# A fused attention and feed-forward kernel: the third query head's matmuls and rotation stand behind the first score tiles

## The reference

```
q = (layernorm(x) @ wq)      # 32 query heads of 128
k, v = ctx @ wk, ctx @ wv    # 8 key/value heads, each shared by 4 query heads
q, k = rope(q), rope(k)      # x * cos + rotate_half(x) * sin
attn = softmax(q @ k.T / sqrt(128) + mask)
x = x + (attn @ v) @ wo
```

## Time and profile before

| | |
|---|---|
| median of 3 runs | 760.55 us (760.4 to 761.59) |
| profiled execution, own time | 761.71 us |
| its span, first to last instruction | 759.7 us |
| mean granted TensorE clock | 0.966 of full speed |
| TensorE matmul busy | 686.3 us, 90% of the span |
| VectorE busy | 546.6 us, 72% |
| ScalarE busy | 365.8 us, 48% |
| GpSimd busy | 434.2 us, 57% |
| span covered by the attention | about 233 to 650 us |

### The profile page before, as it was taken

The page is one execution under the profiler, slowest core; times in us unless marked ns, Lnnn a source line. Parts: engine busy times, 40 slices in busy tenths (PEclk is TensorE's granted clock), DMA queues, the critical chain, the costliest instruction groups (busy, mean ns, idle before and its releaser), DMA issues.

```text
span 759.7 us, 10849 instructions
## 1 busy us (share of the span) xinstructions
PE 686.3 (90%) x3104; PEld 500.8 (66%) x3104; DVE 546.6 (72%) x1057; ACT 365.8 (48%) x685; POOL 434.2 (57%) x387
## 2 busy tenths in 40 slices
PE   4699679797766899999999999999999999599998
PEld 1244234344335678888888888888888888478886
DVE  6877629978785788888888888787888887631112
ACT  1277404246332675656666666566666564031111
POOL 1655505383243786667666766667676544536672
PEclk9899879899998999999999999999999999899999
DMA  8744504321400122121211212212112002203221
GB/s 335 258 146 130 186 1 138 104 78 56 152 28 28 57 98 69 57 70 41 82 42 57 81 39 86 68 42 59 66 41 83 28 15 98 83 2 121 86 83 55
DMA packets 37162, 63.58 MB, mean 84 GB/s; under 512 B 3216, under 2 KB 11536, under 8 KB 36112
## 3 DMA queue, kind: packets, MB, share of 16 engines
q1 hardware_dynamic: 37136, 63.26, 25.8%
HBM read 53.81 MB, written 9.44 MB: 83 GB/s over the span
## 4 chain that ended last, share of the span: by engine, by line
PE 73%; DVE 17%; issue 5%; ACT 3%; POOL 1%; DMA 1%; POOLq 0%; ACTq 0%; DVEq 0%
PE ps L502 15%; PE ps L504 15%; PE ps L503 15%; PE ps L564 10%; PE ps L531 7%; PE ps L409 5%; DVE mx_amax L1041 2%; DVE mx_raw L1054 2%; PE ps L459 1%; DVE f L1083 1%; DVE f_amax L1078 1%; DVE stats L962 1%; PE ps L385 1%; DVE k_cos L1073 1%; PE ps L418 1%
## 5 line engine op out<-in xcount | busy, mean ns | idle before, releaser
L888 POOL TENSOR_SCALAR prob<-prob,rinv 128x512 f32<-128x512 f32 x128 | 89.0, 696 | 122.3 <-DVE rinv L1198 122.2
L754 ACT ACTIVATE prob<-ps,nmax 128x512 f32<-128x512 f32 x128 | 88.3, 690 | 62.8 <-DVE nmax L1191 60.5
L765 ACT CAST pT<-ps 128x512 fp32r<-128x512 f32 x128 | 75.1, 587 | 81.5 <-PE ps L531 80.7
L564 PE MATMUL ps<-xt,wq_sb 128*128 128x512 f32 x384 | 106.0, 402 | 6.1 <-DVE q_cos L1206 3.0
L1191 DVE CUSTOM_DVE_ANT_0 ps<-ps,mask_sb 128x512 f32<-128x512 f32 x128 | 88.3, 690 | 17.7 <-PE ps L504 16.7
L409 PE MATMUL ps<-ctxT,wk_sb 128*128 128x512 f32 x128 | 66.6, 679 | 28.1 <-DVE k_cos L1073 14.1
L1212 DVE TENSOR_TENSOR pT<-ps,pT 128x512 fp32r<-128x512 f32 x128 | 86.9, 679 | 4.7 <-ACT pT L765 1.7
L564 PEld LDWEIGHTS ps<-xt,wq_sb 128*128 128x128 f32 x384 | 73.6, 193 | 24.6 <-issue 5.5
L531 PE MATMUL ps<-idf,prob 128*128 128x128 f32 x512 | 76.6, 272 | 0.0
L531 PEld LDWEIGHTS ps<-idf,prob 128*128 128x128 f32 x512 | 64.0, 142 | 16.2 <-POOL prob L888 0.4
L409 PEld LDWEIGHTS ps<-ctxT,wk_sb 128*128 128x128 f32 x128 | 27.2, 219 | 62.9 <-issue 56.3
(11 more groups left out here) (147 smaller groups left out, 1607.5 us busy)
## 6 DMA issues: line engine op xcount, KB each, us to landing
mx_raw<-in_mxw SPq DMA_DIRECT2D x8, 1024.0 KB, 6.3
wq_raw<-in_wq SPq DMA_DIRECT2D x32, 256.0 KB, 3.2
wo_raw<-in_wo SPq DMA_DIRECT2D x32, 256.0 KB, 2.6
k_scr<-k_cos SPq DMA_DIRECT2D x16, 256.0 KB, 6.5
v_scr<-v_st SPq DMA_DIRECT2D x16, 256.0 KB, 6.8
kr<-k_scr SPq DMA_DIRECT2D x16, 256.0 KB, 2.8
vr<-v_scr SPq DMA_DIRECT2D x16, 256.0 KB, 3.9
ffn_raw<-in_gate_w SPq DMA_DIRECT2D x11, 256.0 KB, 2.7
```

The lines of the kernel that those rows point to most:

```text
L564: last = mm(query_bank(H), wq_sb[:, par, l, k], xt[:, r, k], start=(n == 0), stop=(n == 11))
L754: nc.scalar.activation(prob[:, j], bank(j % 2), ACT.Exp, bias=nmax[:, j:j + 1], scale=-1.0, accum_out=rsum[:, j:j + 1]).then_inc(exps, 1)
L765: copy(pT[:, v % 2, 0, :, i * P:(i + 1) * P], bank(2 + i % 2).rearrange("p (k c) -> p k c", k=4)).then_inc(ph_ready, 1)
L888: nc.gpsimd.tensor_scalar(prob[:, i], prob[:, i], rinv[:, i:i + 1], 1.0, ALU.mult, ALU.mult).then_inc(probs, 1)
```

## The change

In unit -1 TensorE no longer makes head 2. Head 2's first 4 matmuls stand behind score tile 0, its other 8 behind score tile 1. Head 3's 12 matmuls stand together at the end of unit 0. In unit 0 the rotation of head 2 moves: ScalarE's swap, VectorE's cosine and GpSimd's sine from `j = 0` to `j = 2`, VectorE's addition from `j = 1` to `j = 2`, the copies to `qt` from `j = 2` to `j = 3`, and GpSimd's split of head 4's weights from `j = 1` to `j = 2`. All other units are as they were, and the number of operations is the same.

```diff
--- before.py
+++ after.py
@@ -582,14 +582,25 @@
                 if hh == 1:
                     last.then_inc(proj_sums, 1)
 
+            def first(U):
+
+                return isinstance(U, int) and U == 0
+
             def unit(U, u, g):
                 for j in range(4):
                     if j % 2 == 1:
                         project(U, u, j)
                     score(U, u, j, g)
+                    if first(U) and j < 2:
+                        for part in range(3 * j // 2 + 1, 2 * j + 2):
+                            query(-1, 3, part)
                     turn_probs(U, u, j)
                     weigh(U, u, j, g)
-                    query(U, u, j)
+                    if first(U) and j == 3:
+                        for part in range(1, 4):
+                            query(U, u, part)
+                    elif not first(U) and (not isinstance(U, int) or U != -1):
+                        query(U, u, j)
                     if j % 2 == 0:
                         project(U, u, j)
 
@@ -765,8 +776,9 @@
                 copy(pT[:, v % 2, 0, :, i * P:(i + 1) * P], bank(2 + i % 2).rearrange("p (k c) -> p k c", k=4)).then_inc(ph_ready, 1)
 
             def unit(U, u, g):
+                late = isinstance(U, int) and U == 0
                 for j in range(4):
-                    if j == 0 and within(U + 2, NH):
+                    if j == (2 if late else 0) and within(U + 2, NH):
 
                         H = U + 2
                         act.wait_ge(q_sums, H + 1)
@@ -780,7 +792,7 @@
                         copy(oT[:, u % 2, 0], bank(4 + u % 2)).then_inc(oh_ready, 1)
                     probs_high(U, u, j)
                     exponent(U, u, j)
-                    if j == 2 and within(U + 2, NH):
+                    if j == (3 if late else 2) and within(U + 2, NH):
 
                         H, par = U + 2, (u + 2) % 4
                         act.wait_ge(q_roped, H + 1)
@@ -886,11 +899,11 @@
                         pool.wait_ge(inverse, 4 * V + i + 1)
                         pool.sem_inc(pool_past_wait, 1)
                         nc.gpsimd.tensor_scalar(prob[:, i], prob[:, i], rinv[:, i:i + 1], 1.0, ALU.mult, ALU.mult).then_inc(probs, 1)
-                    if j == 0 and within(U + 2, NH):
+                    if j == (2 if late else 0) and within(U + 2, NH):
                         pool.wait_ge(q_swapped, U + 3)
                         tt(q_swp[:].rearrange("p (b c) -> p b c", b=BATCH), q_swp[:].rearrange("p (b c) -> p b c", b=BATCH),
                            ropeQ[:, 1].unsqueeze(1).to_broadcast([P, BATCH, SEQ]), ALU.mult).then_inc(q_sined, 1)
-                    if j == 1 and within(U + 4, NH):
+                    if j == (2 if late else 1) and within(U + 4, NH):
                         H, par = U + 4, u
                         load = g * 2 + (u + 4) // 2 + 1
                         pool.wait_ge(wq_in[par % 2], 16 * load)
@@ -1211,11 +1225,11 @@
                         dve.wait_ge(ph_ready, 4 * V + i + 1)
                         tt(pT[:, v % 2, 1, :, i * P:(i + 1) * P], bank(2 + i % 2).rearrange("p (k c) -> p k c", k=4),
                            pT[:, v % 2, 0, :, i * P:(i + 1) * P].bitcast(F32), ALU.subtract).then_inc(p_split, 1)
-                    if j == 1 and within(U + 2, NH):
+                    if j == (2 if late else 1) and within(U + 2, NH):
                         dve.wait_ge(q_sined, U + 3)
                         dve.wait_ge(q_cosed, U + 3)
                         tt(q_cos[:], q_cos[:], q_swp[:], ALU.add).then_inc(q_roped, 1)
-                    if j == 2 and within(U + 2, NH):
+                    if j == (3 if late else 2) and within(U + 2, NH):
                         par = (u + 2) % 4
                         dve.wait_ge(qh_ready, U + 3)
                         tt(qt[:, par // 2, par % 2, 1], q_cos[:], qt[:, par // 2, par % 2, 0].bitcast(F32), ALU.subtract).then_inc(q_split, 1)
```

## The result

The changed kernel takes 764.88 us (median of 6 runs, 764.21 to 765.68), the kernel before 760.73 us in the 6 runs beside them (760.13 to 761.59). The ratio is 1.005, 95% interval 1.004 to 1.0061: 4.15 us slower where 1.0 us was forecast, and outside the range of 759.7 to 762.9. The sign was right, the size was not.

A forecast was written before the change was run, and what follows sets the result against it. TensorE bounds the saturated stretch, entered when VectorE's lead-in chain through head 3's cosine allows. A row maximum 0.51 us late plus a 0.51 us uncovered copy gave 760.55 + 1.02 = 761.6 us, range 759.7 to 762.9.

The forecast's parts named there:

- What bounds the kernel: TensorE bounds units of 12.77 us from about 269 us; the lead-in hangs on head 3's cosine, the mark to follow.
- Step 1: Lead-in, early score tiles: 0 us gained, since row maximum 0 waits behind VectorE's low part of head 1, staying at 248.17.
- Step 2: Lead-in, tile 2 no longer behind head 3's matmuls: row maximum 2 at 250.93, 0.74 us gained for the moment.
- Step 3: Head 2's rotation between row maxima 2 and 3: VectorE waits 1.7 us for the sine, row maximum 3 0.51 late.
- Step 4: ScalarE's high part of head 2, now behind exponential 3, delays head 3's swap: 0.51 us more, cosine at 258.71.
- What else moves, at no cost: Lead-in: low part of head 2 and row maximum 4 come 1.9 to 2.3 us later, covered before head 3's cosine.
- Row maximum 4's delay is handed on: Rival, lead-in: low part 2 and row maximum 4 slip past their slack; loss 1.6 to 2.3 us, chance 0.11.
- The sum: Head 3's cosine 1.02 us late, handed on unchanged through the saturated stretch to the end: 761.6 us, +0.13%.
- The rival on the clock: TensorE idling around 257.4 to 259.5 in the lead-in lowers its clock: 2.8 us more, 764.4 us, chance 0.04.
- the 0.67 us of the other addition: Shorter measured length, beside a GpSimd scaling, weighed for head 2's addition; with it row maximum 3 is 0.09 us late.

The follow-up runs named there:

- a_add_late: The changed kernel with VectorE's addition of head 2 moved from ahead of row maximum 3 to behind it: 762.2 us, ratio 1.0011.
- a_high_first: The changed kernel with ScalarE's high part of head 2 ahead of exponential 3 again: 761.4 us, ratio 1.0011.
- b_late8: The kernel before with 8 extra matmuls (1.8 us, results overwritten) in units 28 and 29: 765.25 us, ratio 1.0053.
- b_late15: The kernel before with 15 extra matmuls (3.4 us, results overwritten) in units 28 and 29: 766.47 us, ratio 1.006.
- b_busy: The kernel before with transposes and matmuls without use filling TensorE's idle time in the lead-in and ahead of the second feed-forward network: 757.90 us, ratio 0.9939.
- a_late7: The changed kernel with 7 extra matmuls (1.6 us, results overwritten) in units 28 and 29: 764.71 us, ratio 1.0047.
- a_again: The changed kernel run again unaltered, beside new runs of the kernel before: 763.84 us, ratio 1.0038.
- a_values_late: The changed kernel with VectorE's low part of the values in unit 1 moved behind row maximum 5: 764.58 us, ratio 1.0054.
- r_busy: The changed kernel, idle TensorE filled, head 2's addition behind row maximum 3, sine ahead of tile 1's scaling, values' split ahead of the high part: 756.95 us, ratio 0.9943.

## Why the prediction was wrong in size and right in sign

**What bounds the kernel**: right. Head 3's cosine was the mark that moved, and a unit still takes 12.77 us.

**Step 1**: right. The early tiles gave nothing; row maximum 0 moved by the 0.20 us that everything ahead of it had moved.

**Step 2**: right, 251.19 less the 0.20 us is 250.99, against 250.93.

**Step 3**: right. VectorE waited 1.61 us for the sine (1.7 forecast), the addition took 1.09 us beside GpSimd's weight split, and row maximum 3 stood at 254.98 less the offset (254.90). a_add_late took the wait away and gained 1.31 us at the cosine.

**Step 4**: right. The high part at 256.63 is behind exponential 3, and a_high_first took back 0.51 us, the size of the term. Both together were 1.10 us at head 3's cosine instead of 1.02.

**What else moves, at no cost**: wrong by one instruction. The text had row maximum 4 late by 1.9 to 2.3 us and covered, and so it came. But it followed only VectorE's queue to head 3's cosine, not reciprocal 3, scaling 3 and the sine, which hang on that row maximum, and gave the values' low part behind the cosine no thought. That one lies on the chain too, and the sine now covered its start: 0.45 us. The rival "Row maximum 4's delay is handed on", given 0.11, had the mechanism (a later sine, a longer VectorE operation), and its lower edge of 1.6 us is nearly the 1.55 of the lead-in, but it looked for it at the low part of head 2 and row maximum 4. There is nothing to see: head 2's low part took 0.69 us (257.27) and row maximum 4 0.69 us (257.88), and VectorE still waited 0.34 us in front of the cosine.

**The sum** is the step that failed: "From there the order is the old one and VectorE's queue runs without a gap to 263.05, so the 1.02 us reaches the saturated stretch and the end." Neither half held. The lateness was 1.55 us on entering the saturated stretch, since the queue had no gap but an instruction of 1.14 us in place of 0.68. And behind that stretch there is a stage whose own length depends on the granted clock, where an arrival 1.78 us later (0.20 and 1.55 of it told above) became 3.98 us. The rival on the clock had nearly the right time, 764.4 us, for the wrong place: it set the fall in the lead-in, and was given 0.04. In the lead-in of the profiled execution the clock was no different from before; that its time was nearly met is luck. Such falls do happen, in the traces of b_late8, b_late15, a_high_first, a_add_late and b_busy between 243 and 261 us, but in kernels with either lead-in. That the clock can be the larger term was in the profile of the kernel before, where it fell near 658.9, inside 6.65 us of idle TensorE; I had read the windows of the lead-in only.

**What stays open**: why the clock falls earlier or later in one execution than in another, and so why the groups of runs are filled so differently. In no profile of the changed kernel with its idle time left in did the short stretch occur except in a_late7. The fall was near 658.9 before and near 659.2 in the changed kernel, so it did not follow the attention's end, which came 1.8 us later; in b_late8 and a_late7 it came later. That the lead-in is worth 1.4 to 1.7 of the 4.15 us is shown by the marks and by the pair with the idle time filled. The 2.19 us behind the attention are shown for the profiled execution, and all five traces with the lead-in changed and no work added have the long stretch; that it comes in every execution, and that a later arrival brings the short one back, is not shown (for the second there is a_late7 alone, and b_late15 against it). a_again, at 3.0 us (ratio 1.0038, 1.002 to 1.0056), shows how far the total itself moves.

## What to carry to other kernels

Where an edit moves a moment by a microsecond, follow it to the end of the program and not only into the next saturated stretch: a later place where the clock falls in TensorE's idle time can be worth more than the edit. Here 1.78 us on arrival became 3.98. Compare such variants with the clock held, by work without use in the idle time, and judge parts of an edit by marks in the trace. When an instruction moves by half a microsecond, look at what GpSimd runs at its new start before its old duration is used again; this goes for instructions that merely follow the edit as well.

## What the runs showed of the hardware

In these traces a VectorE operation of 128x512 that reads two tensors from SBUF and starts while GpSimd is in an operation takes the rest of that operation and 0.55 us more. For the values' low part, the rest and the duration were 0.11 and 0.68 us (before), 0.26 and 0.82 (a_high_first), 0.55 and 1.10 (a_values_late, beside a weight split), 0.59 and 1.14 (changed), 0.92 and 1.47 (a_add_late), 1.05 and 1.60 (r_busy). Head 2's addition in the changed kernel fits: the weight split beside it had 0.56 us left at 254.16, and it took 1.09. From 250 us on, some 90 such operations in the trace of each of before, changed, a_add_late and r_busy keep to it within 0.03 us. The Trainium skill, SBUF — State Buffer, section SBUF: two separate sides, has the reason: the port pair that VectorE and GpSimd share is an exclusive lock for a whole instruction, and who starts second is blocked. The trace agrees: the duration grows by as much as the rest does. By it, the 0.67 us of the other addition is the case where VectorE was first, and GpSimd's scaling beside it the one that was blocked: 0.38 us of the addition were left at its start, and it took 0.93 us, again 0.55 more. Had I used it for every two-input operation on the chain instead of for one, the forecast would have been a loss of about 1.5 us (an estimate, 1.02 + 0.46), and still 2.7 us short.
